# VectorE waits for its own last instruction between the three maps of sums, differences and low parts

## What is computed

```
out_normal = conv3x3(x, w_normal)
offset     = concat(conv3x3(x, w_offx), conv3x3(x, w_offy))        # 9 taps, dy and dx each
out_x      = deform_conv(x, offset, w_dx)                          # 9 taps, bilinear samples of x
out_y      = deform_conv(x, offset, w_dy)                          # same samples, other weights
out        = relu(bn1(conv3x3(concat(out_normal, out_x, out_y), w_fusion)))
result     = relu(bn2(conv3x3(out, w_conv2)) + x)
```

## Time and profile before

| | |
|---|---|
| median of 3 runs | 2672.19 us (2653.64 to 2672.3) |
| the profiled execution | 2661.92 us, span 2660.1 us |
| PE busy | 2361.2 us (89%) |
| VectorE busy | 2252.6 us (85%) |
| GpSimd busy | 2000.7 us (75%) |
| ScalarE busy | 1565.6 us (59%) |
| DMA queue of the gathers | 58.8% of 16 engines |
| granted TensorE clock, mean | 0.966 |

### The profile page before, as it was taken

One profiled execution on the slowest core, in us unless ns is written; L12 is line 12 of the kernel. 1 busy time (PEld: TensorE's weight loads), 2 busy tenths in 40 slices (PEclk: granted clock), 3 DMA queues, 4 the chain that ended last, 5 costly groups with the idle time before them and its releaser, 6 DMA issues.

```text
span 2660.1 us, 46973 instructions
## 1 busy us (share of the span) xinstructions
PE 2361.2 (89%) x15680; PEld 2323.2 (87%) x15680; DVE 2252.6 (85%) x5999; ACT 1565.6 (59%) x3577; POOL 2000.7 (75%) x1807
## 2 busy tenths in 40 slices
PE   3667899998999989989999999999989999899897
PEld 3567888998999989989899998998989988888897
DVE  5788888888998988988888898998888888888862
ACT  5777877877655555655555555555555555555531
POOL 7777777777777777777777777777777777777740
PEclk9879999999999999999999999999999999999999
DMA  7766777777777777777777777766666666666640
GB/s 223 214 213 211 241 229 222 227 226 222 220 226 241 220 227 232 228 233 233 233 231 240 239 238 225 234 206 206 200 205 195 207 197 204 198 196 206 194 126 25
DMA packets 179139, 564.89 MB, mean 212 GB/s; under 512 B 32721, under 2 KB 34129, under 8 KB 178769
## 3 DMA queue, kind: packets, MB, share of 16 engines
q0 software_dynamic: 144000, 471.97, 58.8%
q1 hardware_dynamic: 34896, 89.91, 9.6%
HBM read 527.41 MB, written 34.34 MB: 211 GB/s over the span
## 4 chain that ended last, share of the span: by engine, by line
DVE 38%; PE 26%; ACT 12%; DMA 11%; issue 9%; POOL 4%; ACTq 0%; DVEq 0%; POOLq 0%; SPq 0%
DVE mixed L756 9%; DMA cells<-slope_table,index 9%; DVE d_lo_f L832 6%; PE work L388 6%; PE work L391 5%; DVE d_lo L708 5%; PE work L394 5%; DVE samp L762 5%; DVE samp_lo L708 5%; ACT samp L535 4%; POOL cells L350 4%; ACT samp_hi L534 3%; DMA cells<-in_xpair,index 3%; PE turned L431 2%; PE acc L388 2%
## 5 line engine op out<-in xcount | busy, mean ns | idle before, releaser
L350 POOL DMA_INDIRECT cells<-slope_table,index x1350 | 1489.7, 1103 | 411.7 <-issue 208.8
L535 ACT ACTIVATE samp<-mixed,wgt 128x128 f32<-128x128 f32 x1800 | 649.1, 397 | 602.8 <-DVE mixed L756 600.0
L756 DVE SCALAR_TENSOR_TENSOR mixed<-cells,wgt 128x256 f32<-128x256 f32 x1350 | 575.6, 476 | 158.4 <-DMA cells<-slope_table,index 155.8
L350 POOL DMA_INDIRECT cells<-in_xpair,index x450 | 501.3, 1114 | 148.9 <-issue 86.3
L388 PE MATMUL work<-d_hi,w_hi 128*128 128x320 f32 x1440 | 480.9, 334 | 75.4 <-ACT off_s L534 73.6
L762 DVE SCALAR_TENSOR_TENSOR samp<-mixed,wgt,samp 128x128 f32<-128x128 f32 x1800 | 515.3, 345 | 29.8 <-ACT samp L535 29.3
L391 PE MATMUL work<-d_lo,w_hi 128*128 128x320 f32 x1440 | 464.4, 322 | 0.0
L394 PE MATMUL work<-d_hi,w_lo 128*128 128x320 f32 x1440 | 463.7, 322 | 0.0
L388 PE MATMUL acc<-samp_hi,w_hi 128*128 128x320 f32 x1440 | 451.3, 313 | 0.0
L391 PE MATMUL acc<-samp_lo,w_hi 128*128 128x320 f32 x1440 | 448.3, 311 | 0.0
L394 PE MATMUL acc<-samp_hi,w_lo 128*128 128x320 f32 x1440 | 447.3, 311 | 0.0
(11 more groups left out here) (86 smaller groups left out, 4198.5 us busy)
## 6 DMA issues: line engine op xcount, KB each, us to landing
cells<-slope_table,index POOLq DMA_INDIRECT x1350, 3.9
slope<-in_xpair SPq DMA_DIRECT2D x54, 384.0 KB, 5.3
slope_table<-slope SPq DMA_DIRECT2D x54, 384.0 KB, 4.1
x_raw<-in_xflat SPq DMA_DIRECT2D x40, 410.0 KB, 4.6
resid<-in_x SPq DMA_DIRECT2D x40, 320.0 KB, 5.2
out<-resid SPq DMA_DIRECT2D x40, 320.0 KB, 4.1
cells<-in_xpair,index POOLq DMA_INDIRECT x450, 3.9
w_lo_f<-in_weights SPq DMA_DIRECT2D x4, 576.0 KB, 8.6
```

The costliest lines, as they stand in the source:

```text
L350: eng.indirect_dma_start(out=cells[:, g, :], out_offset=None, in_=cell_rows, in_offset=bass.IndirectOffsetOnAxis(ap=index[:, par, j, k:k + ...
L535: return eng.activation(dst, src, ACT.Copy, scale=scale)
L756: eng.scalar_tensor_tensor(out=both, in0=corner[:, g, :, 1, :], scalar=wgt[:, par, 1, 0, j, k:k + 1], in1=base, op0=ALU.mult, op1=ALU.add, ...
```

## The change

VectorE gets waits on its own semaphores. In `sums` and `zs` it waits in front of each map until the last instruction of the map before has completed; so in `sums_low` and `zs_low`, where the semaphore now rises once per map (TensorE's thresholds are three times as high in turn, for the same moment). In front of `mid`'s low part it waits until the last instruction of `zs` has completed. No instruction that computes is added, removed or moved. In front of the first map each wait is for something of the strip before.

```diff
                             if q == 0:
                                 at_least(eng, w_lo_done, 1 + W_FUSE)
-                                at_least(eng, sums_low_done, i - 1)
+                                at_least(eng, sums_low_done, 3 * (i - 1))
                             if q == 2:
-                                at_least(eng, zs_low_done, i - 1)
+                                at_least(eng, zs_low_done, 3 * (i - 1))
                                 at_least(eng, f_one, i - 1)
@@ def sums
                 for g in range(3):
                     even, odd = (raw[:, g].rearrange("p (i z) w -> p i z w", z=2)[:, :, z, :] for z in range(2))
                     to = d_raw[:, g, :, 1:1 + W]
+                    at_least(eng, sums_done, 6 * s + 2 * g)
@@ def zs
                 for g in range(3):
                     to = d_raw[:, g, :, 1:1 + W]
+                    at_least(eng, zs_done, 7 * s + 2 * g)
@@ def sums_low
                 for g in range(3):
+                    at_least(eng, sums_low_done, 3 * s + g)
                     for first in (SUM_ROW, DIFF_ROW):
                         rows = slice(first, first + PAIRS)
                         ins = low(d_lo[:, g, rows, 1:1 + W], d_raw[:, g, rows, 1:1 + W], d_hi[:, g, rows, 1:1 + W])
-                ins.then_inc(sums_low_done, 1)
+                    ins.then_inc(sums_low_done, 1)
@@ def zs_low
                 for g in range(3):
+                    at_least(eng, zs_low_done, 3 * s + g)
                     for rows in (slice(0, HR), slice(HR, Z_ROWS - 1)):
                         ins = low(d_lo[:, g, rows, 1:1 + W], d_raw[:, g, rows, 1:1 + W], d_hi[:, g, rows, 1:1 + W])
-                ins.then_inc(zs_low_done, 1)
+                    ins.then_inc(zs_low_done, 1)
@@ step, VectorE
                             if fl.fuse:
                                 at_least(eng, mid_hi_done, s + 1)
+                                at_least(eng, zs_done, 7 * min(s + 2, NS))
```

## The result

The changed kernel takes 2595.4 us (median of 4 runs, 2595.06 to 2602.97) against 2669.56 us (median of 4; the table in front had three of them); the ratio is 0.9741 with a 95% interval of 0.9698 to 0.9784. So it is 2.6% faster; the medians alone lie 74 us, or 2.8%, apart. Its profiled execution took 2602.97 us, the slowest of its four, so the two profiled executions lie only 59 us apart.

A forecast was written before the change was run, and what follows sets the result against it. It took GpSimd's 1800 gathers, some held by VectorE's unbroken runs, to bound the kernel. Of 87 us gained, three quarters, 65 us, count: 2662 - 65 = 2597, said as 2600 us; range 2552 to 2665.

The forecast's parts named there:

- GpSimd is last, and its length is made of gathers and a fixed pause: GpSimd's 2543.1 us stretch is 1990.75 us busy plus 552 us of issuing pauses, 0.307 us per gather, with no real waiting.
- An emptied VectorE lets a held gather in: In `sums` and `zs`, a real wait empties VectorE after each pair; a gather is held at most 0.88 or 0.71 us.
- Rival (a): In `sums` and `zs` the waits let no gather in; VectorE's 45 us stay hidden: 2667 us, no change; chance 0.12.
- That a gather gets in when VectorE's unbroken run ends: Beside `sums` and `zs`, gathers get in at the end of VectorE's two-input run, finishing 0.82 us behind it.
- GpSimd's gain: Shorter holds of gathers beside `sums` and `zs` save GpSimd 87 us, bounds 0 and 170.
- VectorE's cost: Each real wait costs VectorE 0.125 us of lost overlap and pause: 45 us for 360, bounds 14 to 54.
- Three quarters of the gain arrive: Over the whole run, 65 us of GpSimd's 87 reach the time, since PE or VectorE becomes last in some strips.
- the sign that I had named for (b): Idle over 0.31 us before gathers, with GpSimd waiting for `mixed` or PE.
- Rival (b): PE and VectorE take over from freed gathers; a third of the gain arrives, 2633 us; chance 0.12.
- Rival (c): VectorE's own path decides, so nine tenths of its 45 us come on top: 2702 or about 2710 us; chance 0.10.
- The number: The forecast time of the changed kernel, 2600 us, said between the two references.
- The sum proper: 2662 - 65 = 2597 us for the whole kernel, against the profiled execution.

The follow-up runs named there:

- e12_load3: The kernel before plus three unread GpSimd memsets in a row at nine places per strip: 2738.09 us, ratio 1.0238.
- e3_met: The changed kernel with all nine waits per strip in place, but for the value reached one strip before, so already met: 2665.39 us, ratio 0.997.
- the rows under 2: Timeline rows of the kernel before: VectorE goes on behind `sums` and `mid` without a break, the next instructions starting 0.08 us before these end.
- e1_maps: The changed kernel without the waits of the low parts, keeping five per strip in `sums`, `zs` and before `mid`'s low part: 2578.25 us, ratio 0.964.
- e2_low: The changed kernel with only the four waits per strip in `sums_low` and `zs_low`: 2687.3 us, ratio 1.0061.
- e8_low_each: The kernel before with ten waits per strip in `sums_low` and `zs_low`: 2678.39 us, ratio 1.0029.
- e7_samp: e1_maps plus one wait per tap, VectorE waiting for its own fifth `mixed` before the first `samp`: 2582.42 us, ratio 0.966.
- e5_load_before: The kernel before plus six small unread GpSimd memsets per strip between gathers: 2698.37 us, ratio 1.0118.

## Why the prediction was right, point by point

**GpSimd is last, and its length is made of gathers and a fixed pause: right.** This was the step on which all hung, against GpSimd's 75% on the page. That busy and idle time add up to the stretch holds for any engine; what carries the step is that the idle time is no wait. Of the 1800 pauses before, 14 are over 0.35 us, and `e12_load3` and the table bear it out.

**An emptied VectorE lets a held gather in: right**, and `e3_met` shows that inside `sums` and `zs` a wait must empty it to do so. Rival (a) falls with it. The rule of the Trainium skill, "SBUF — State Buffer", section "Who interferes with whom", is that the blocked engine waits until the other's instruction finishes. It describes the changed kernel no better than the one before: at 1328.18 the gather got in behind the pair, not behind the first instruction.

**That a gather gets in when VectorE's unbroken run ends: right for the pairs, not as a rule.** What I took for the end of a run (1352.83, 1368.48) is no break, as the rows under 2 show. And beside `mixed` and `samp` most held gathers get in at the end of an instruction that the next one overlaps. The forecast needed only that none is held past a real wait, and that held: in the changed kernel none in `sums` or `zs` was. I also gave 3.92 us as the longest gather; that is the longest of the 1350 of rows 4, and one of the other 450 took 4.78.

**GpSimd's gain: 87 us forecast, 83.3 measured**, mean gather 1.060 us for "about 1.06". That it came so near is in part luck: inside, the term was put together differently. `zs` gave 74 us (2.08 to 0.24 us per strip) and `sums` 21 (1.13 to 0.60), 95 together, where I had booked 87 for both. Some 12 us were lost again beside other instructions; the largest shifts are `samp`, up from 42 to 83 us of hold, and `mixed`, down from 83 to 51. I had not seen that holds move.

**VectorE's cost: 0.125 us per wait, right.** `sums` takes 2.74 us with two waits, 2.49 without: 0.125 each. The Trainium skill, "VectorE: DVE Perf Modes", section "The DRAIN you can't avoid", has a semaphore after each instruction as free. For waits that are met `e3_met` agrees (1.99 us for six of `zs`, as in rows 6). For a wait on the instruction just issued the measurement contradicts it: 0.125 us.

**Three quarters of the gain arrive: right in sum, by a share that I had guessed.** The stretch fell by 62 us of 83 (the medians by 74), and VectorE's and ScalarE's waits for cells to 65 us, where 61 were forecast. What I did not say is where the missing quarter goes: the waits in the low parts, which I had priced at 20 us of VectorE with nearly nothing to win, cost 17 us of the result (`e1_maps`). In the kernel before, four such waits left GpSimd's idle time as it was (`e2_low`). Here they bring 14 us of it, 580.7 against 566.9: the gain has brought the engines nearly level. This is the sign that I had named for (b): the median pause stayed at 0.305 us, but 33 pauses in place of 14 are over 0.35 us, and the mean of all is 0.32 in place of 0.31. Rival (b) was thus a true part of the outcome, at a quarter of the gain, and the whole of what `e7_samp` could win.

**Rival (c), VectorE's path decides in the kernel before: refuted** by `e8_low_each`, though `e2_low` by itself looked like it.

**The number:** 2600 forecast, 2595.4 measured. The sum proper was 2597 against a profiled execution of 2661.92; there 2602.97 came, a gain of 59 us for 65. Between these and the medians' 74 us lies only the spread of single executions, so a fit closer than some 10 us is luck.

## What to carry to other kernels

Look at the duration of each GpSimd indirect DMA against its median before judging GpSimd by its busy share: a pause that never varies and gathers held behind VectorE's back-to-back instructions make an engine at 75% the last one. Break such runs by a wait of VectorE for its own last instruction, only where the trace shows gathers held to the end of a run; each wait costs 0.12 us. In this kernel five per strip (2578 us) beat two or three at one of the two places alone (2623 and 2614 us), nine with four where no gather was held for long (2595 us), and twelve (2610 us). Two places with holds cannot be priced apart, since a gather freed in one runs into another: measure them together.

## What the runs showed of the hardware that was not expected

A gather held by VectorE ends 0.82 us behind the end of a VectorE instruction: to within 0.02 us in 71 of the 76 gathers over 1.9 us before, and in 37 of 38 in the changed kernel. Back-to-back scalar_tensor_tensor with both inputs in SBUF hold it past instruction after instruction, in `zs` and `mid` through up to nine (3.72 us in rows 7); six tensor_tensor of the same size seldom do (1.23 us in rows 8). One instruction alone holds it to its end, tensor_tensor too. The longest gather before, and the instruction beside it (GpSimd, then VectorE; 133.41 is 0.82 us behind 132.59):

```profile
128.63 4.78 POOL L350 DMA_INDIRECT cells<-in_xpair,index  x1 [0.30 <-issue]
...
127.63 4.96 DVE L708 TENSOR_TENSOR w_lo<-w_lo_f,w_hi 128x4608 fp32r<-128x4608 f32 x1 [3.12 <-ACT w_hi L534]
```

Why scalar_tensor_tensor and tensor_tensor differ, and why a gather gets in between `mid` and `mixed` but not between two instructions of `zs`, was not tried. A met wait alone doesn't let it in: 38 of 40 strips of `e3_met` still have the long gather in `zs`, and the one at 2225.26 was held past the met waits in front of `samp`. A GpSimd memset of 0.17 us between two gathers lengthens the way from one to the next by just 0.024 us, from 0.305 to 0.329 (`e5_load_before`).
